# A fused AdaLN block with a selective scan: the C/B projection as four column tiles

## The reference, cut to what matters

```python
x_ssm, z = jnp.split(x @ w_in.T + b_in, 2, axis=-1)
dt = jax.nn.softplus(x_ssm @ w_dt.T + b_dt)
Bm = x_ssm @ w_B.T + b_B          # 16 columns
Cm = x_ssm @ w_C.T + b_C          # 16 columns
# at each token, for D = 512 channels and N = 16 states:
h = exp(A * dt) * h + dt * Bm * x_ssm
y = sum(h * Cm over N)
```

## Time and profile before

| | |
|---|---|
| median of 3 runs | 4576.69 us (4574.44 to 4577.13) |
| the profiled execution | 4574.68 us, of which the span from first to last instruction is 4572.9 us |
| PE busy | 4356.8 us, 95% of the span |
| ACT, DVE, POOL busy | 3814.2, 3698.9, 3596.2 us (83%, 81%, 79%) |
| mean granted clock of TensorE | 0.99 |

### The profile page before, as it was taken

How to read it: one execution, slowest core, us unless ns; L and a number is a source line. 1 busy time by engine, 2 the same in 40 slices (tenths; PEclk the granted TensorE clock), 3 DMA queues, 4 the chain that set the end, 5 groups by cost and what they waited for, 6 DMA issues and landing times. The chain is left out here.

```text
span 4572.9 us, 69933 instructions
## 1 busy us (share of the span) xinstructions
PE 4356.8 (95%) x22528; PEld 2784.8 (61%) x22528; DVE 3698.9 (81%) x5132; ACT 3814.2 (83%) x6371; POOL 3596.2 (79%) x1999
## 2 busy tenths in 40 slices
PE   7999999999999999999999999999999999999997
PEld 3666666666666666666666666666666666666664
DVE  3778888888888888888888888888888888888885
ACT  3788888888888888888888888888888888888885
POOL 3787878887878877877878878878788878788784
PEclk8999999999999999999999999999999999999999
DMA  4233233333233333332333333332333333333322
GB/s 138 73 79 87 81 89 82 85 81 88 80 94 81 83 88 87 85 87 77 86 93 83 89 82 84 83 90 78 91 76 89 87 86 86 86 77 89 86 77 58
DMA packets 177763, 388.89 MB, mean 85 GB/s; under 512 B 22693, under 2 KB 22693, under 8 KB 177402
## 3 DMA queue, kind: packets, MB, share of 16 engines
q1 hardware_dynamic: 140538, 250.19, 17.4%
q0 software_dynamic: 36864, 134.23, 15.3%
HBM read 215.50 MB, written 34.63 MB: 55 GB/s over the span
## 5 line engine op out<-in xcount | busy, mean ns | idle before, releaser
L379 POOL TENSOR_TENSOR work<-work,c_bc 128x1024 f32<-128x1024 f32 x1024 | 2463.3, 2418 | 765.9 <-DVE work L1140 676.7
L1140 DVE TENSOR_TENSOR_SCAN work<-work,state,b_ps 128x512 f32<-128x512 f32 x1792 | 2257.7, 1274 | 301.1 <-PE b_ps L468 272.7
L852 ACT ACTIVATE work<-u_td,b_td 128x512 f32<-128x512 f32 x2048 | 1453.2, 710 | 163.7 <-PE b_ps L468 158.3
L842 ACT ACTIVATE work<-dt_t,neg_a 128x512 f32<-128x512 f32 x2048 | 1451.3, 709 | 4.7 <-DVE work L1140 4.4
L468 PE MATMUL b_ps<-ident,work 128*128 128x128 f32 x8192 | 1253.3, 276 | 65.0 <-DVE work L1140 57.1
L468 PEld LDWEIGHTS b_ps<-ident,work 128*128 128x128 f32 x8192 | 974.8, 142 | 505.3 <-issue 303.2
L543 PEld LDWEIGHTS y_ps<-ident,work 128*128 128x128 f32 x6144 | 740.0, 142 | 481.7 <-issue 466.0
L543 PE MATMUL y_ps<-ident,work 128*128 128x128 f32 x6144 | 862.8, 273 | 1.6 <-DMA work<-work 1.3
L692 PE MATMUL dense<-h_t,w_in_t 128*128 128x512 f32 x1024 | 514.5, 599 | 1.1 <-DVE u_td L1223 1.1
L600 PE MATMUL dense<-w_out_t,proj 128*128 128x512 f32 x1024 | 509.9, 595 | 0.0
L658 PE MATMUL dense<-xs_t,w_dt_t 128*128 128x512 f32 x1024 | 501.2, 593 | 0.0
(11 more groups left out here) (115 smaller groups left out, 4530.4 us busy)
## 6 DMA issues: line engine op xcount, KB each, us to landing
c_bc<-c_d SPq DMA_DIRECT2D x512, 256.0 KB, 3.3
work<-work POOLq DMA_DIRECT2D x256, 512.0 KB, 5.6
xn<-in_x SPq DMA_DIRECT2D x128, 256.0 KB, 5.1
x<-in_x SPq DMA_DIRECT2D x128, 256.0 KB, 4.3
out_dram<-x SPq DMA_DIRECT2D x128, 256.0 KB, 4.4
work<-in_wmod SPq DMA_DIRECT2D x2, 1024.0 KB, 6.5
w_in_t<-in_w_in_t SPq DMA_DIRECT2D x2, 1024.0 KB, 9.9
gain_shift<-par_d SPq DMA_DIRECT2D x8, 256.0 KB, 6.0
```

What stands on the lines that cost most here:

```text
L379: gp.tensor_tensor(made_here, both(hs, HS_RING, s * U + i), c_bc[:, (s * N + n) % C_RING:(s * N + n) % C_RING + 1, :].to_broadcast([P, 2, ...
L842: A(decay[:, (s * U + i) % DEC_RING, :], dt_t[:, s % 2, j, :], ACT.Exp, scale=neg_a[:, j, n:n + 1]).then_inc(S["dec_done"], 1)
L852: A(v[:, n % V_RING, tb, :], u_td[:, tb, :], ACT.Copy, scale=b_td[:, s % 2, tb, n:n + 1]).then_inc(S["v_done"], 1)
L1140: V.tensor_tensor_scan(hs[:, (s * U + i) % HS_RING, :], decay[:, (s * U + i) % DEC_RING, :], b_ps[:, i % 2, :], state[:, i:i + 1] if s % N ...
```

## The change

The product for C and B is computed in four column tiles. Tile tb holds the 32 weight columns in array columns 32 tb to 32 tb + 31, takes the 128 tokens of block tb, and writes partitions 32 tb to 32 tb + 31 of the bank's first 128 columns. So 16 matmuls of 128 columns take the place of 4 of 512. The evacuation on ACT becomes 128 x 128 instead of 32 x 512, with the bias loaded four times, once into each quarter of the partitions. One 128x128 transpose gives B by tokens, in place of four of 32 rows. C goes to DRAM in four stores instead of one. In the cost table `cb` goes from 1 to 0.4 and `bt` from 0.5 to 0.2, so TOTAL goes from 96.9 to 94.2.

```diff
--- before.py
+++ after.py
@@ -51,7 +51,7 @@
         z.2.0 ut.0 z.2.1 z.2.2 ut.1 z.2.3
         s.0 ut.2 s.1 s.2 ut.3 s.3
         z.3.0 z.3.1 z.3.2 z.3.3""".split()
-    LENGTH = dict(yz=0.6, xt=0.6, x2=0.6, ut=0.6, bt=0.5, res=0.5)
+    LENGTH = dict(yz=0.6, xt=0.6, x2=0.6, ut=0.6, bt=0.2, cb=0.4, res=0.5)
     GROUPS = ("g", "pre.0", "pre.1", "pre.2", "pre.3", "z.0", "xs.0", "xs.1", "xs.2", "xs.3", "dt.0", "dt.1", "dt.2",
               "dt.3", "cb", "z.1", "z.2", "s", "z.3")
     BEGIN, END = {}, {}
@@ -112,7 +112,7 @@
         b_z = sb("b_z_col", [P, KD])
         b_dt = sb("b_dt_col", [P, KD])
         d_skip = sb("d_skip_col", [P, KD])
-        b_cb = sb("b_cb_col", [2 * N, 1])
+        b_cb = sb("b_cb_col", [P, 1])
         neg_a = sb("neg_a", [P, KD, N])
         w1 = sb("w1", [P, J])
         b1 = sb("b1", [P, J])
@@ -134,7 +134,7 @@
         dt_t = sb("dt_t", [P, 2, KD, T])
         y_sb = dt_t[:, :, :, :].rearrange("p c k t -> p c (k t)").rearrange("p c (b d) -> p c b d", b=TB)
         u_td = sb("u_td", [P, TB, D])
-        cb_t = sb("cb_t", [2 * N, T])
+        cb_t = sb("cb_t", [P, P])
         b_td = sb("b_td", [P, 2, TB, N])
         sz_t = sb("sz_t", [P, KD, T])
         proj = sb("proj", [P, KD, T])
@@ -175,13 +175,14 @@
             return dn[(GROUPS.index(".".join(str(n) for n in group)) + s + 1) % 2]
 
         N_LATE = 6 + 5 * 2 + 2
+        N_WD = 4 + TB
         once = """wx_loaded wd_loaded late_loaded b2_loaded const_zeroed const_masks neg_done scal_done w2top_done
         w2dg_done b_out_loaded bout_done moved_ps moved c_exp c_one c_rcp silu_c rows_ps rows_taken mods_ps mods_done sign_done gate_done par_made
         par_stored gs_loaded wg_loaded wout_done""".split()
 
 
         PER = {
-            "SP": dict(stored_0=Q, stored_1=Q, stored_2=Q, stored_3=Q, c_stored=Q),
+            "SP": dict(stored_0=Q, stored_1=Q, stored_2=Q, stored_3=Q, c_stored=TB * Q),
             "Pool": dict(prod_done=U // 2, skip_added=KD // 2, xsh_done=TB, x1_done=TB, dt_done=KD, u_done=KD, sz_done=KD),
             "PE": dict(b_made=U, y_added=len(ADDS), s_ps=1, g_used=J, yz_ps=KD, out_ps=TB, res_used=TB, pre_ps=TB, xt_ps=KD, xs_ps=KD,
                        cb_ps=1, bt_ps=1, x2_ps=KD, dt_ps=KD, z_ps=KD, ut_ps=TB),
@@ -258,7 +259,8 @@
             load("wd_loaded", w_dt[:, :, :], blocks("w_dt_t"))
             load("wd_loaded", w_cb[:, :, :], blocks("w_cb_t"))
             load("wd_loaded", b_dt[:, :], ap["b_dt_c"])
-            load("wd_loaded", b_cb[:, :], column("b_cb"))
+            for tb in range(TB):
+                load("wd_loaded", b_cb[tb * 2 * N:(tb + 1) * 2 * N, :], column("b_cb"))
             load("wd_loaded", neg_a[:, :, :], ap["A_log_c"])
             for n in range(2, 6):
                 load_part(n)
@@ -299,7 +301,7 @@
 
             def spread_c(k, n):
                 if n == 0:
-                    sp.wait_ge(S["c_stored"], at("c_stored", k, Q))
+                    sp.wait_ge(S["c_stored"], at("c_stored", k, TB * Q))
                 if n >= C_RING:
                     sp.wait_ge(S["prod_done"], at("prod_done", k, (n - C_RING + 1) * KD // 2))
                 else:
@@ -330,7 +332,9 @@
                     if has_f and i == made("cb", 3) + 2:
                         sp.wait_ge(S["cb_done"], at("cb_done", f, 1))
                         sp.wait_ge(S["prod_done"], at("prod_done", f - 2, U // 2))
-                        sp.dma_start(c_d[f % 2], cb_t[0:N, :]).then_inc(S["c_stored"], Q)
+                        for tb in range(TB):
+                            sp.dma_start(c_d[f % 2][:, tb * P:(tb + 1) * P], cb_t[tb * 2 * N:tb * 2 * N + N, :]
+                                         ).then_inc(S["c_stored"], Q)
                     if s == 0 and i == 17:
                         store_gates()
                     if has_s and s % NC == 0 and i == 40:
@@ -647,7 +651,7 @@
 
             def add_dt(s, f, b, m, k):
                 if m == 0:
-                    pe.wait_ge(S["wd_loaded"], 5 * Q)
+                    pe.wait_ge(S["wd_loaded"], N_WD * Q)
                     pe.wait_ge(S["xs_done"], at("xs_done", f, k + 1))
                 if k == 0:
                     pe.wait_ge(S["h2_done"], at("h2_done", b, m + 1))
@@ -663,16 +667,16 @@
             def add_cb(s, f, k):
                 if k == 0:
                     pe.wait_ge(S["vabs_done"], at("vabs_done", f, 3))
-                last = mm(long(s, "cb")[0:2 * N, :], w_cb[:, k, :], xs_t[:, k, :], start=(k == 0), stop=(k == KD - 1))
+                for tb in range(TB):
+                    last = mm(long(s, "cb")[tb * 2 * N:(tb + 1) * 2 * N, 0:P], w_cb[:, k, :],
+                              xs_t[:, k, tb * P:(tb + 1) * P], start=(k == 0), stop=(k == KD - 1),
+                              tile_position=(0, tb * 2 * N))
                 if k == KD - 1:
                     last.then_inc(S["cb_ps"], 1)
 
             def turn_b(s, f):
                 pe.wait_ge(S["cb_done"], at("cb_done", f, 1))
-                for tb in range(TB):
-                    last = nc.tensor.transpose(inside(s, "z.1")[:, tb * 2 * N:(tb + 1) * 2 * N],
-                                               cb_t[:, tb * P:(tb + 1) * P], ident[0:2 * N, 0:2 * N])
-                last.then_inc(S["bt_ps"], 1)
+                turn(inside(s, "z.1")[:, 0:P], cb_t[:, :]).then_inc(S["bt_ps"], 1)
 
             def add_z(s, f, b, m, k):
                 if k == 0:
@@ -858,7 +862,7 @@
 
             def decay_rates():
                 yield 39
-                act.wait_ge(S["wd_loaded"], 5 * Q)
+                act.wait_ge(S["wd_loaded"], N_WD * Q)
                 A(neg_a[:, :, :], neg_a[:, :, :], ACT.Exp).then_inc(S["neg_done"], 1)
 
             def relu(c, j):
@@ -967,7 +971,7 @@
                 act.wait_ge(S["cb_ps"], at("cb_ps", f, 1))
                 act.wait_ge(S["c_stored"], at("c_stored", f, 0))
                 act.wait_ge(S["bt_ps"], at("bt_ps", f, 0))
-                A(cb_t[:, :], long(s, "cb")[0:2 * N, :], ACT.Identity, bias=b_cb[:, :]).then_inc(S["cb_done"], 1)
+                A(cb_t[:, :], long(s, "cb")[:, 0:P], ACT.Identity, bias=b_cb[:, :]).then_inc(S["cb_done"], 1)
                 yield made("bt", 0)
                 act.wait_ge(S["bt_ps"], at("bt_ps", f, 1))
                 A(b_td[:, f % 2, :, :],
@@ -1202,7 +1206,7 @@
                 for m in range(KD):
                     yield made("dt", m, 3)
                     bank = long(s, "dt", m)
-                    dve.wait_ge(S["wd_loaded"], 5 * Q)
+                    dve.wait_ge(S["wd_loaded"], N_WD * Q)
                     dve.wait_ge(S["dt_ps"], at("dt_ps", f, m + 1))
                     dve.wait_ge(S["dec_done"], at("dec_done", b, U))
                     dve.wait_ge(S["yz_ps"], at("yz_ps", b, KD))
```

## The result

The changed kernel takes 4713.2 us (median of 4 runs, 4711.21 to 4713.91), against 4576.42 for the kernel before (4574.44 to 4577.13): a ratio of 1.030, with a 95% interval of 1.0286 to 1.0314. The profiled execution took 4712.81 us, so a chunk costs (4712.81 - 4574.68) / 31 = 4.46 us more on the mean.

What follows compares the result with a forecast made beforehand. It took POOL, not PE, to bound the end of the chunk. On 4574.7 us came 2.8 to 2.9 us a chunk, about 90, and 65 for the clock: 4730 us, range 4600 to 4770.

Steps and rivals of the forecast that it cites:

- net of what moved in (13.66 and 1.72): tv(49) to `ut.0`: 16.9 us, less the old stretch of 13.66 and 1.72 of PE work formerly ahead: +1.5 a chunk.
- `cb` for one k: Tiled product for C and B: 0.55 us each k, between 0.22 with all tiles together and 0.87 if they queue.
- `z.0.3`, tv(28): tv(28) needs scan 26, 3.7 us after the `z.0.3` matmul, with 2.6 of PE work ahead: stall +1.1 us a chunk.
- `dt.0.3`, tv(43): Two passes and a scan after `dt.0.3` take 2.9 us, against 2.15 of PE work ahead of tv(43): +0.8 a chunk.
- `z.2.3`, `ut.2`: A scan, zc2 and zm2 take 2.6 us, against 2.17 of PE work ahead of `ut.2`, a slot earlier: +0.4 a chunk.
- `g.3`: It moves behind the last additions to `y_ps`, into a gap set by DVE before `res.0`: -0.86 us a chunk.
- smaller waits: Waits at `xt.1`, `x2.0` and `out`, between -0.4 and +0.3 us, taken as -0.1 a chunk.
- clock: PE's clock falls to half in the wait before nearly every `z.2.1`: 2.1 us a chunk, 65 us in all.
- POOL's chain: End of step: dtadd2 and product(52) come between product(48) and u3, so `ut.0` is late and PE stands 5.1 us.
- that the clock holds: Rival: all as forecast but without the loss of 65 us to half speed: 4665 us, chance 17%.
- That only the chain grows: Rival: only POOL's stretch lengthens and DVE stalls vanish into slack: 4620 us, down to 4575; chance 14%.
- That POOL is in time: Rival: u3 ends early enough that PE never waits: 4515 us, or 4475 with four tiles at once; chance 13%.

Runs made afterwards that it cites:

- e4: The changed kernel with POOL's additions and multiplications for dt.2 and dt.3 one slot earlier: 4635.1 us.
- e7: The changed kernel, new cost table included, with POOL's additions and multiplications for dt.2 and dt.3 together in slot 50, ahead of product(50): 4494.8 us.
- e2: The kernel before with only the new cost table: 4684.55 us.
- e3: The changed kernel with five useless 128x512 matmuls ahead of the wait of `ut.0` in each step: 4647.35 us.
- e8: e1 with three useless 128x512 matmuls ahead of the wait of `ut.0` in each step: 4569.93 us.
- e5: e1 with POOL's addition and multiplication for dt.3 together in slot 50, ahead of product(50): 4514.88 us.
- e6: The kernel before with only the edit of POOL's program from e5: 4566.49 us.
- e9: e5 with the first step of ACT's sigmoid for z.1 one slot later: 4513.42 us.
- e1: The changed kernel with the cost table of before, leaving the tiles, the one transpose and the four stores: 4630.36 us.

## Why the prediction was right, point by point

The main mechanism held, and so did nearly every step, each with its size. In us for the chunk shown:

| step of the forecast | predicted | measured after |
|---|---|---|
| tv(49) to product(48) | 2.1 | 2477.45 - 2475.35 = 2.10 |
| tv(49) to `ut.0` | 16.9 | 2491.89 - 2475.35 = 16.54 |
| net of what moved in (13.66 and 1.72) | +1.5 | +1.16 |
| PE stands at `ut.0` | 5.1 (3.7 to 6.4) | 5.55 |
| `cb` for one k | 0.55 (0.22 to 0.87) | 0.27 |
| `bt` | 0.11 | 0.11 |
| `z.0.3`, tv(28) | +1.1 | +1.18 |
| `dt.0.3`, tv(43) | +0.8 | +0.87 |
| `z.2.3`, `ut.2` | +0.4 | +0.40 |
| `g.3` | -0.86 | fits in for nothing |
| smaller waits | -0.1 | -0.2 |
| clock | 2.1 | 2.04 |

Rows of the timeline of PE after, behind the first `ut.0` of the chunk (at 2349.15) and for the steps away from it:

```profile
2350.06 1.92 PE L696 MATMUL dense<-h_t,w_in_t 128*128 128x512 f32 x2
2351.77 1.06 PE L472 MATMUL b_ps<-ident,work 128*128 128x128 f32 x4
2352.62 1.34 PE L696 MATMUL dense<-h_t,w_in_t 128*128 128x512 f32 x2
2353.79 0.60 PE L547 MATMUL y_ps<-ident,work 128*128 128x128 f32 x4
...
2358.54 0.66 PE L472 MATMUL dense<-ident,xn 128*128 128x128 f32 x4 [0.24 <-DVE tmp L1242]
...
2376.14 1.47 PE L547 MATMUL y_ps<-ident,work 128*128 128x128 f32 x12
2384.38 0.63 PE L597 MATMUL dense<-ident,h_t 128*128 128x128 f32 x4 [0.27 <-DVE proj L1182]
2385.82 0.66 PE L472 MATMUL dense<-ident,dt_t 128*128 128x128 f32 x4 [0.38 <-ACT gm L894]
...
2429.61 1.10 PE L633 MATMUL dense<-h_t,w_in_t 128*128 128x512 f32 x2 [0.53 <-ACT h_t L860]
2432.77 0.63 PE L472 MATMUL b_ps<-ident,work 128*128 128x128 f32 x4 [0.31 <-DVE work L1144]
...
2461.42 0.66 PE L472 MATMUL b_ps<-ident,work 128*128 128x128 f32 x4 [0.71 <-DVE work L1144]
```

- **POOL's chain** was right in its order and its size. The 16.54 and the wait of 5.55 are both within 0.5 of the forecast. The forecast's "without a wait" overlooked the two gaps of 0.30 at the transfers, which POOL has before and after alike, so the difference of the two stretches is not touched. e4 and e7 show that the chain is the cause: take work out from in front of u3, and the time returns.
- **`g.3`** behaves as the forecast said. The additions end at 2376.14 + 1.31 = 2377.45, and `res.0` starts 6.93 later, against 6.92 before, with `g.3` now inside.
- **The shifted slots** appear as forecast. The first has a part that the forecast didn't name: `xs.0.0` itself starts 0.70 late, in a wait that the trace puts down to ACT (0.53 in the row). tv(28) then adds 0.48, and the sum is the 1.18. e2 shows these stalls without any tile, and e7 shows them still there (101.9) in the fastest kernel.
- **The smaller waits** were forecast at -0.1 and came to -0.2. In slots 6 to 12 they grow by 0.6, with a new one at `yz.1` for ACT (0.38 in the row, 0.54 from start to start), and by 0.2 at `z.3.0`. They shrink by 0.6 at `x2.0`, by 0.3 at `xt.1` and by 0.1 at `xt.0`. No experiment takes these apart. The wait of `x2.0` before, which is gone after:

```profile
2377.08 0.63 PE L468 MATMUL dense<-ident,xn 128*128 128x128 f32 x4 [0.36 <-ACT xs_t L964]
```

- **`cb`** was mis-sized: "If all four tiles stream together, two passes remain, 0.22. I take the middle, 0.55". The four tiles do stream together. A k takes 0.27, and `cb` as a whole 2479.80 - 2478.04 - 0.43 = 1.33 instead of 4.1. The saving is 2.8, not 1.5. The Trainium skill (TensorEngine Tiling (Array Packing), Key Properties) says that different tiles can load and multiply in parallel, and the 0.27 agrees with it. The time hardly depends on this term, as the forecast said of the opposite case: what is saved ahead of `ut.0` is waited for at `ut.0`.
- **The clock** was right: 2.04 in the chunk, from the four stretches of work behind its first `ut.0` (2349.15 to 2353.79) that take 0.47, 0.85, 0.41 and 0.31 longer than at full speed. Behind the next `ut.0` the same four lose 2.35. By e3 it is 64 us in all, against 65 forecast. That it fits so closely is in part luck: the 4.2 us at half speed were "somewhat more" than those of a single fall, chosen and not worked out. By the rule of the Trainium skill (TensorE: Matmul & The Clock Gate, Part 1), half clock after an idle gap, this was due in each chunk. The granted clock of 0.50 in the window from 2490 agrees, and so does its absence in e3, where the useless matmuls leave a gap of only some 1.3 us.
- **The stores** cost nothing that a wait shows, and e8, which has them and loses nothing, bears this out.
- **The rivals**: that the clock holds fell with the 0.50. That only the chain grows fell with tv(28) and tv(43). That POOL is in time fell with the wait of 170.7. The case that it describes, the changed kernel with POOL in time, was made by hand in e7. With four tiles at once, as they turned out to work, the forecast had 4475 us for it, and e7 took 4494.8.

The terms as measured sum to 1.16 + 1.18 + 0.87 + 0.40 - 0.86 - 0.2 + 2.04 = 4.6, while this chunk lost 4.82 and the mean chunk 4.46. The 0.2 between the first two is not taken apart. Of the mean, a part is known: the first two chunks lost only 2.4 and 3.3 us, by the starts of their `ut.0`. The forecast's own sum was 4.95. It was 0.3 too high at `ut.0`, and each other term was within 0.1.

## What to carry to other kernels

Where a table of costs sets the order of instructions, a truer cost is a change to the program of every engine. Check what the new order puts ahead of each instruction that another engine waits for, even if the engine itself is far from full (POOL is busy 76% and sets the end of the stretch). Ahead of such a wait, time saved on PE only makes the wait longer, and it can cost the clock besides; first bring the releasing engine's work forward (e7: 4713 to 4495), and only then does the saving arrive. When a wait is taken away, look for the next one right behind it before counting the gain (e5, e6 and e9 each met one).

## What the runs showed of the hardware

- Four column tiles of 32 columns work at the same time in f32 too. In the changed kernel 24 records of 128 columns take 0.82 us, 34 ns a record, where a full-width transpose of 128 columns takes 108 ns a record (four in 0.43). Changes of tile included, the product takes 1.33 us in four tiles and took 4.1 in one.
- PE's clock falls at the wait of nearly each chunk (3.93 us in e1, 5.55 in the changed kernel), in the wait or, in the chunk shown of e1, within a microsecond behind it. Each fall costs about 2 us of the work behind it. Useless matmuls in the wait make the kernel faster: 64 us with 4.3 us of them a chunk (e3), 61 us with 2.6 (e8 against e1).
- Half speed shows plainly in the length of a record group, not only in the clock: 3.58 us in e1 for four records that take 1.88 otherwise.
